# The last 1x1 convolution of a two-layer block, done by pairs of quarters, with its half group as two 64-row products

## The reference

```python
# layer 0, per 8x8 window
y = affine(conv1x1(x, fc1_w, fc1_b), fc1_s, fc1_t)
idx = knn_idx(nodes, 9)                       # nearest nodes by normalised distance
feat = concat([x_i, x_j - x_i]); h = gelu(bn(feat @ ew)); h = max over the 9 neighbours
x1 = affine(conv1x1(h, fc2_w, fc2_b), fc2_s, fc2_t) + x
# layer 1
h = relu(_bn(einsum('oc,bchw->bohw', w1, x1), ...))        # 96 -> 576 channels
h = relu(_bn(depthwise 3x3 of h with wd, ...))             # 576 channels
out = x1 + _bn(einsum('oc,bchw->bohw', w2, h), ...)        # 576 -> 96 channels
```

## Time and profile before

| what | value |
|---|---|
| median of 3 runs | 4085.38 us (4085.14 to 4087.81) |
| profiled execution | 4088.99 us, of which span 4087.1 us |
| busy PE / DVE / ACT / POOL | 95% / 93% / 90% / 23% |
| mean granted PE clock | 0.987 of full |
| L579, the full groups of w2 | x2048, 497.4 us busy |
| L581, the half group of w2 | x512, 153.6 us busy |
| L791, res, by ACT | x256, 470 ns each (median) |

### The profile page before, as it was taken

How to read it: one execution, slowest core, us unless ns; L and a number is a source line. 1 busy time by engine, 2 the same in 40 slices (tenths; PEclk the granted TensorE clock), 3 DMA queues, 4 the chain that set the end, 5 groups by cost and what they waited for, 6 DMA issues and landing times.

```text
span 4087.1 us, 79112 instructions
## 1 busy us (share of the span) xinstructions
PE 3900.1 (95%) x22752; PEld 2050.5 (50%) x22752; DVE 3821.1 (93%) x5162; ACT 3698.3 (90%) x6806; POOL 931.4 (23%) x1060
## 2 busy tenths in 40 slices
PE   6999999999999999999999999999999999999984
PEld 3445555455555555555554555545555455555442
DVE  3699999999999999999999999999999999999996
ACT  4899999899998999999999999989999899999983
POOL 1122222222222222222222222122222122222113
PEclk9999999999999999999999999999999999999996
DMA  2133333333433333342333333333342333333333
GB/s 60 24 65 71 67 76 65 72 62 66 79 62 67 63 77 66 65 84 50 79 69 67 67 74 66 64 72 70 59 85 54 68 69 68 78 64 58 62 66 65
DMA packets 100116, 272.34 MB, mean 67 GB/s; under 512 B 14946, under 2 KB 23394, under 8 KB 93476
## 3 DMA queue, kind: packets, MB, share of 16 engines
q0 software_dynamic: 65536, 184.58, 26.4%
q1 hardware_dynamic: 34116, 82.27, 7.5%
HBM read 77.68 MB, written 25.69 MB: 25 GB/s over the span
## 4 chain that ended last, share of the span: by engine, by line
PE 70%; DVE 10%; ACT 9%; issue 9%; DMA 1%; ACTq 0%; POOL 0%; DVEq 0%; POOLq 0%; SPq 0%
PE pg L651 18%; PE pmisc L579 9%; PE pg L654 9%; PE pvu L638 8%; PE pmisc L565 7%; DVE acc L1043 7%; PE pmisc L522 3%; PE pmisc L515 2%; PE pvu L624 2%; ACT MV L813 2%; PE pmisc L581 2%; PE pmisc L545 2%; DVE hid L1021 2%; PE pmisc L550 2%; ACT tapped L850 1%
## 5 line engine op out<-in xcount | busy, mean ns | idle before, releaser
L1043 DVE SCALAR_TENSOR_TENSOR acc<-hpad,w,acc 128x1024 f32<-128x1024 f32 (+1 forms) x2304 | 2615.8, 1159 | 34.6 <-issue 17.5
L651 PE MATMUL pg<-MV,VU 128*128 128x512 f32 x2048 | 1150.6, 644 | 40.5 <-ACT VU L821 29.7
L830 ACT ACTIVATE g<-pg 128x512 f32<-128x512 f32 x1536 | 913.2, 595 | 131.3 <-PE pg L654 81.2
L1021 DVE TENSOR_REDUCE hid<-g 128x192 f32<-128x1536 f32 x512 | 891.9, 1742 | 0.0
L430 POOL DMA_DIRECT2D acc<-tapped x256 | 240.9, 941 | 2108.5 <-DVE acc L1043 1824.3
L813 ACT ACTIVATE MV<-pvu,cst 64x512 f32<-64x512 f32 x1024 | 696.5, 680 | 11.9 <-PE pvu L624 5.0
L579 PE MATMUL pmisc<-acc,w 128*96 128x256 f32 x2048 | 497.4, 386 | 50.5 <-ACT acc L860 35.4
L654 PE MATMUL pg<-MV,VU 128*64 128x512 f32 x2048 | 527.7, 592 | 0.0
L565 PE MATMUL pmisc<-x,w 96*128 96x512 f32 (+1 forms) x1024 | 515.4, 605 | 8.8 <-ACT hpad L772 8.8
L638 PE MATMUL pvu<-wVU,y 97*64 97x192 f32 x4096 | 447.4, 340 | 22.0 <-ACT MV L813 21.7
L579 PEld LDWEIGHTS pmisc<-acc,w 128*96 128x96 f32 x2048 | 331.5, 165 | 263.8 <-issue 155.9
(11 more groups left out here) (102 smaller groups left out, 4447.8 us busy)
## 6 DMA issues: line engine op xcount, KB each, us to landing
acc<-tapped POOLq DMA_DIRECT2D x256, 512.0 KB, 4.9
xin<-in_x_dram SPq DMA_DIRECT2D x32, 768.0 KB, 5.7
invb<-rows_dram SPq DMA_DIRECT2D x32, 768.0 KB
x<-in_x_dram POOLq DMA_DIRECT2D x128, 192.0 KB, 4.1
res<-x POOLq DMA_DIRECT2D x128, 192.0 KB, 5.1
out_dram<-res SPq DMA_DIRECT2D x128, 192.0 KB, 3.2
hpad<-hpad SPq DMA_DIRECT2D x112, 33.0 KB, 1.8
g<-in_consts_dram SPq DMA_DIRECT2D x1, 640.0 KB
```

The costliest lines, as they stand in the source:

```text
L651: last = nc.tensor.matmul(ps[:, :], VU[:, r, part, 0:ONE128], cols[part], start=True, stop=True)
L830: nc.scalar.activation(g[:, p % 2, part, :, :], pg[(3 * p + part) % 2][:, :].rearrange("p (n k) -> p n k", k=KN), ACT.Gelu).then_inc(gelu_ ...
L1021: nc.vector.tensor_reduce(hid[:, c % 2, j, :, :], g[:, r], op=ALU.max, axis=AX.X).then_inc(hid_ready, 1)
L1043: nc.vector.scalar_tensor_tensor(out=dst, in0=src, scalar=wk, in1=dst, op0=ALU.mult, op1=ALU.add).then_inc(tap_done, 1)
```

## The change

`W2_AT` is now `{12: 0, 15: 1}`: quarters 0 and 2 are two jobs at offset 12, quarters 1 and 3 at offset 15. So slots with p % 8 = 4 and 7 hold two quarters each, and slots 6 and 0 hold none. Of a pair, the first job issues only its four full products. The second issues its own four, then the half group of both: w2T rows 0 to 63 by acc partitions 0 to 63 into the first job's bank, and rows 64 to 127 by partitions 64 to 127 into its own bank. `misc_ready` counts for both after these. The DMA adds and the stores of both half strips are at offsets 16 and 17 (before: adds at 15 and 17, stores at 16 and 18).

```diff
--- before.py
+++ after.py
@@ -47,14 +47,14 @@
 TAP0_AT = {}
 TAP0_LATE = {0: [0], 1: [1], 3: [2], 4: [3], 5: [4]}
 RELU2_AT = {6: [0], 7: [1], 10: [2, 4], 11: [3]}
-W2_AT = {12: 0, 14: 1, 15: 2, 16: 3}
+W2_AT = {12: 0, 15: 1}
 TAP_COUNTS = [3, 4, 4, 4, 5, 5, 5, 4, 2]
 PRODUCT_AT = {0: 0, 1: 1, 6: 2, 7: 3}
 SUM_AT = {5: (0,), 6: (1,), 9: (2,), 10: (3,)}
 SELF_AT = {2: 'self_half', 3: 'self_full', 4: 'self_half', 5: 'self_full'}
 ORDER = ('ssq', 'fc1', 'inv', 'self_full', 'self_half', 'fc2', 'w1', 'w2')
-ADD_AT = {o + 1: q for o, q in W2_AT.items() if q % 2 == 1}
-STORE_AT = {o + 2: q for o, q in W2_AT.items() if q % 2 == 1}
+ADD_AT = {o + 1: q for o, q in W2_AT.items() if q == 1}
+STORE_AT = {o + 2: q for o, q in W2_AT.items() if q == 1}
 FIRST = [(g, k) for k in range(1, TAPS - 1) for g in (0, 1)]
 SECOND = [(2, 1), (3, 1), (2, 2), (3, 2), (4, 1), (2, 3), (3, 3), (4, 2), (2, 4), (4, 3), (3, 4), (2, 5), (4, 4), (3, 5),
           (2, 6), (4, 5), (3, 6), (2, 7), (4, 6), (3, 7), (4, 7), (4, 8)]
@@ -104,8 +104,8 @@
         bc, c = (b, (p - 5) // 4) if p >= 5 else (b - 1, CHUNKS - 1)
         if valid(bc, B):
             jobs.append(("fc2", bc, c))
-    for _, t, s, fours in due_in(W2_AT, b, p):
-        jobs.append(("w2", t, s, fours))
+    for _, t, s, q in due_in(W2_AT, b, p):
+        jobs += [("w2", t, s, q), ("w2", t, s, q + 2)]
     for _, t, s, parts in due_in(W1_AT, b, p):
         jobs += [("w1", t, s, part) for part in parts if part[1] < 2 or t == 0]
     jobs.sort(key=lambda job: ORDER.index(job[0]))
@@ -381,14 +381,15 @@
                         sp.sem_inc(sp_passed, 1)
                         sp.dma_start(hpad[64:128, gr, 0:2, :], hpad[0:64, gr, 8:10, :]).then_inc(kept_half, 16)
 
-                    for o, t, s, q in due_in(STORE_AT, b, p):
-                        sp.wait_ge(out_sum[q // 2], 16 * (s + 1))
-                        sp.sem_inc(sp_passed, 1)
-                        c = 2 * t + q // 2
-
-                        bs = b if p - o >= 2 * SLOTS else b - 1
-                        sp.dma_start(ov[bs, :, c * CW:(c + 1) * CW], res[:, q // 2, :]).then_inc(
-                            store_done[q // 2], 16)
+                    for o, t, s, _ in due_in(STORE_AT, b, p):
+                        for part in range(2):
+                            sp.wait_ge(out_sum[part], 16 * (s + 1))
+                            sp.sem_inc(sp_passed, 1)
+                            c = 2 * t + part
+
+                            bs = b if p - o >= 2 * SLOTS else b - 1
+                            sp.dma_start(ov[bs, :, c * CW:(c + 1) * CW], res[:, part, :]).then_inc(
+                                store_done[part], 16)
 
             image_loop(sp, image, TAIL)
             for k in range(2):
@@ -486,7 +487,8 @@
                         for gr in groups:
                             add_product(t, s, gr)
                     for o, t, s, q in due_in(ADD_AT, b, p):
-                        add_x1(b, p, o, t, s, q)
+                        for part in (q, q + 2):
+                            add_x1(b, p, o, t, s, part)
                     if p % 16 in XN_AT and valid(bi, B):
                         stationary_copy(bi, 4 * h + XN_AT[p % 16])
                     if p % 4 == 1:
@@ -578,8 +580,13 @@
                     for gr in range(FULL):
                         nc.tensor.matmul(ps[0:C, 0:4 * W], w2T[:, gr, :], acc[:, par, sums_of(gr, q * 4 * W, 4 * W)],
                                          start=(gr == 0), stop=False)
-                    last = nc.tensor.matmul(ps[0:C, 0:4 * W], w2T[:, FULL + q // 2, :],
-                                            acc[:, par, sums_of(FULL, (q % 2) * 4 * W, 4 * W)],
+                    if q < 2:
+                        return
+                    upper = pmisc[bank_of(b, p, k - 1)]
+                    half = sums_of(FULL, (q % 2) * 4 * W, 4 * W)
+                    nc.tensor.matmul(upper[0:C, 0:4 * W], w2T[0:64, FULL, :], acc[0:64, par, half],
+                                     start=False, stop=True).then_inc(misc_ready, 1)
+                    last = nc.tensor.matmul(ps[0:C, 0:4 * W], w2T[64:128, FULL + 1, :], acc[64:128, par, half],
                                             start=False, stop=True)
                 last.then_inc(misc_ready, 1)
 
```

## The result

The changed kernel takes 4210.3 us (median of 4 runs, 4208.8 to 4219.9); the kernel before, on the same chip, 4086.1. The ratio is 1.0308 with a 95% interval of 1.029 to 1.0326: slower by 124 us. The forecast was 4220, with a range of 4125 to 4280.

What follows compares the result with a forecast made beforehand. PE and ACT, slot by slot, were taken to bound the kernel. 30 × 1.43 + 31 × 3.27 − 9.4 = +134.9 us on the profiled 4089.0 gave 4223.9, about 4220 by the median; range 4125 to 4280.

Steps and rivals of the forecast that it cites:

- PE's own stream: PE's products: +1.88 us per pair slot, 2.16 freed per emptied slot, −0.56 us per strip.
- the turn: Array switching from 128 rows to 64, once per pair: 0.15 us taken, bounds 0 and 0.5.
- Rival 3: The 64-row half products don't overlap: 122 × 0.43 = +52 us, 4272 us; chance 12%.
- Slots 6 and 0 give little back: Slots losing their quarter wait on ACT; with pair slots, +1.43 or +3.27 us per strip, by strip kind.
- the loop over ACT: Gather 2, then ACT from GELU 2 to MV, then PE's values and gather 2; 5.29 us from GELU 2 to MV's end.
- Rival 1: Slots are pooled and PE's stream decides: 34 us faster, 4051 us; chance 11%.
- Adds and stores, cost 0: Moving POOL's adds and SP's stores to offsets 16 and 17 was to cost 0.
- The clock, rival 4: PE's clock falls in the new stalls of slots 14 and 16: 2.8 us per strip, 171 us, 4391; chance 4%.
- The terms of the strips: 30 strips as p = 4 to 8 at +1.43 us, 31 as p = 12 to 16 at +3.27.
- Signs named ahead: Profile values expected after the change: slot lengths, PE's waits for MV, DVE's wait for scores, starts of L587 and L589.

Runs made afterwards that it cites:

- experiment 3: Second ReLU of group 1 cut to 64 of 1024 columns: in the changed kernel 4153.6 us, in the kernel before 4086.6 us.
- Experiment 5: The kernel before with the store of the first half strip at offset 17 instead of 16, nothing else: 4062.8 us, ratio 0.9942.
- changed, shorter ReLU: The changed kernel with the second ReLU of group 1 over 64 of its 1024 columns: 4153.6 us, ratio 1.0166 to the kernel before.
- the wait filled: The changed kernel with five products of constants ahead of the values in slots with p % 8 = 0: 4199.4 us.
- the held bank: The kernel before, first quarter's bank held until the second quarter's slot: 4044.8 us with 64-row half products, 4074.0 with 128-row ones.

## Why the prediction was right, and where its sizes were off

**PE's own stream.** A pair slot was to cost +1.88 us and cost 1.90 in slots 4, 12, 15, 20 and 28 alike (medians over 14 images). The row halves overlap fully, as assumed from the column halves. For the turn 0.15 us was taken and 0.17 is paid, though not where the prediction had it: half of it lies between the two passes of the pair. Rival 3 (no overlap) is out: L587 and L589 start together.

**Slots 6 and 0 give little back.** Forecast for slots 14 to 16 with slot 12: +3.27 per strip; measured 1.90 − 0.08 − 0.39 + 1.90 − 0.06 = 3.27. Forecast for slots 4 to 8: +1.43; measured 1.90 − 2.16 + 2.56 − 0.94 + 0.03 = 1.39. The reason given, the loop over ACT from GELU 2 to MV, is shown by experiment 3 for slots 8 and 16, and for 6 and 14 by the waits of the trace. Rival 1 (PE's stream decides) is out: PE's stream is shorter and the time longer.

**Adds and stores, cost 0.** This step failed. I looked at who waits for the moved DMAs and not at what SP does next, once its store is out: a load of 768 KB that met the jump of the loop in the kernel before and doesn't now. Slots 31, 0 and 1 were forecast at +15.9 us over 14 images and came to −2.2, which is 18 us in the change's favour. Of these, 13 us are the shorter stalls (22.1 us together before, 8.7 after), and the clock makes up most of the rest: it fell at all six stalls before and at one now, against three new falls in slots 0. Experiment 5 shows that this store alone is worth 23 us in the kernel before.

**The clock, rival 4.** It was priced at 2.8 us in every strip and given 4%. It did happen, in ten places at 1.5 to 1.6 us: the seven in slots 16 put slots 16 to 19 11 us above the forecast over 14 images, and filling the wait takes 11 us back. The reason given against it, that the waits are little more than half as long as the stall of the loop, was no sufficient one.

−18 and +11 leave −7 us over the loop; it was +114.5 instead of +122.2 there. Outside its 14 images the step was +6.8 instead of +12.7, which was not followed further. Profile against profile the forecast of +134.9 thus was 13.6 us too high, and by the medians 10 us. The terms of the strips were right; that the total came so near is in part luck, since two errors had opposite signs.

**Signs named ahead.** Waits for MV in slots 14 and 16 (1.5 to 2 us named, 1.70 and 2.03 seen), DVE's wait (300 named, 288 seen), slots 8 and 16 (6.6 and 7.1, both seen) and slot 4 (10) are as said. Slots 6 and 7 are not: 6.6 and 9.9 were named, 5.83 and 10.48 are seen. Their sum is near (16.5 and 16.31): the scores that open slot 7 don't wait for VU, so the time that PE waits for ACT counts to slot 7. From the half products to the values 0.52 us had been taken and it is 0.61, and 0.09 more ahead of them.

## What to carry to other kernels

- Where engines run in lockstep slot by slot, add up the larger of the paths in each slot, not each engine's total. Work that moves from a slot in which it hid beside another engine's loop into one that its own engine bounds costs in full there and returns nothing behind it: here PE had 20 us less to do and the kernel took 124 us longer.
- An idea and its placement are to be timed apart. The 64-row halves are worth 29 us; bringing two quarters together for them cost 166 us. Holding a bank from slot to slot gave the one without the other.
- A change that shortens or lengthens waits of PE can move the falls of its clock too: the −57 us of experiment 3 hold some 15 us of that, the −23 us of experiment 5 some 11. Count the falls in both traces before a difference is put down to the wait.
- When a DMA is moved, look at what stands behind it on the queue that issues it, and at what else in the program wants the DMA engines then.

## What the runs showed of the hardware

- Two products over 64 rows each, in different halves of the array and into different banks, run beside each other with starts within 10 ns. Such a pair costs 0.17 us over one product of 128 rows, 0.09 ahead of it and 0.08 between its two passes. The Trainium skill, "TensorEngine Tiling (Array Packing)", section "Tiling Modes", says that tiles operate independently and that a change of mode drains the engine. The starts agree with the first; of a drain the runs show no more than these 0.17 us.
- Where the loop jumps back PE stands idle, by an amount that follows when a packet of the instruction queue arrives. With a load of 768 KB in flight just ahead (DMA share 0.92 in one window) it was 2.9 to 5.0 us at six places; with the load 25 to 28 us earlier, 1.3 to 1.8 us at all six in the changed kernel, and 1.1 to 1.3 us at four and 2.7 us at two in the kernel before with the later store.
- The granted clock fell behind ten of 25 waits of PE of 2.03 us in the changed kernel, and behind none of its waits of 1.70 us. In other runs shorter ones were enough: once a wait of 1.70 us (changed, shorter ReLU), and stalls from 1.60 us on where the loop starts again (1.60 us with the wait filled, 1.62 with the held bank, 1.79 in the changed kernel). What tells the ones from the others stays open.
